# Local attention: 128-token transposes split into two 64-token ones on the halves of the array's rows, both groups beside the mask, one shared pair of banks

## The reference

```
qkv = shift_tokens(x) @ Wqkv;  q, k, v = split(qkv)
q, k = rope(l2norm(q) * qs), rope(l2norm(k) * ksc)       # per head
sim = q @ k.T * 8, each window of 32 queries sees its own and the previous window
out = softmax(masked sim) @ v;  x = out @ Wo + x
x = (a * gelu(gate)) @ W2 + b2 + x,  a, gate = layernorm(shift_tokens(x)) @ W1 + b1
```

## Time and profile before

| | us |
|---|---|
| median of 3 runs | 5310.74 (5309.5 to 5312.04) |
| profiled execution, span from first to last instruction | 5297.4 |
| TensorE busy | 4675.9 (88%) |
| DVE busy | 4003.6 (76%) |
| ACT busy | 3636.0 (69%) |
| POOL busy | 2657.4 (50%) |

### The profile page before, as it was taken

How to read it: one execution, slowest core, us unless ns; L and a number is a source line. 1 busy time by engine, 2 the same in 40 slices (tenths; PEclk the granted TensorE clock), 3 DMA queues, 4 the chain that set the end, 5 groups by cost and what they waited for, 6 DMA issues and landing times. The chain is left out here.

```text
span 5297.4 us, 148317 instructions
## 1 busy us (share of the span) xinstructions
PE 4675.9 (88%) x45796; PEld 2897.7 (55%) x45796; DVE 4003.6 (76%) x8097; ACT 3636.0 (69%) x11780; POOL 2657.4 (50%) x2108
## 2 busy tenths in 40 slices
PE   5999999698898998989989767989989989899897
PEld 1333332366565665656656544665656656566565
DVE  7888886587786877868778546878868778687785
ACT  1777777586785876858768514867858778587684
POOL 3000000465665666656656404656656566566564
PEclk6999999899999999999999977999999999999998
DMA  0000000222222222222222302222222222222223
GB/s 13 1 2 1 2 1 1 85 59 72 59 59 77 59 71 60 59 77 59 64 66 60 83 7 85 59 73 59 57 78 59 72 62 57 77 60 69 65 56 93
DMA packets 332305, 288.20 MB, mean 54 GB/s; under 512 B 149102, under 2 KB 290964, under 8 KB 329748
## 3 DMA queue, kind: packets, MB, share of 16 engines
q1 hardware_dynamic: 331028, 281.93, 20.6%
q10 hardware_dynamic: 768, 0.02, 0.0%
HBM read 100.42 MB, written 30.41 MB: 25 GB/s over the span
## 5 line engine op out<-in xcount | busy, mean ns | idle before, releaser
L929 POOL TENSOR_TENSOR g_rn<-g_ss,g_minus_half 128x8 f32<-128x8 f32 x384 | 636.8, 1658 | 299.7 <-DVE g_ss L1077 297.0
L929 POOL TENSOR_TENSOR f_rn<-f_ss,f_minus_half 128x8 f32<-128x8 f32 x384 | 636.8, 1658 | 299.2 <-DVE f_ss L1077 295.9
L425 DVE TENSOR_REDUCE a_maxima<-a_max 128x1 f32<-128x512 f32 x1024 | 651.3, 685 | 148.4 <-PE a_max L539 142.2
L1003 ACT ACTIVATE f_ex<-f_bank,f_nmx 128x96 f32<-128x96 f32 x1536 | 501.5, 338 | 226.8 <-DVE f_nmx L1082 226.8
L1003 ACT ACTIVATE g_ex<-g_bank,g_nmx 128x96 f32<-128x96 f32 x1536 | 501.6, 338 | 226.6 <-DVE g_nmx L1082 226.6
L349 ACT ACTIVATE a_pex<-a_scores 128x512 f32<-128x512 f32 x1024 | 531.7, 607 | 159.6 <-PE a_scores L548 159.6
L934 POOL TENSOR_TENSOR f_qr<-f_t 128x512 f32<-128x512 f32 x384 | 488.4, 1272 | 268.8 <-DVE f_t L1100 268.8
L934 POOL TENSOR_TENSOR g_qr<-g_t 128x512 f32<-128x512 f32 x384 | 488.2, 1271 | 269.0 <-DVE g_t L1100 269.0
L1172 PE MATMUL g_bank<-g_wqkv,g_xT 128*128 128x512 f32 x768 | 407.2, 613 | 30.4 <-ACT g_xT L977 24.3
L1172 PE MATMUL f_bank<-f_wqkv,f_xT 128*128 128x512 f32 x768 | 406.4, 612 | 29.2 <-ACT f_xT L977 24.5
L1077 DVE TENSOR_REDUCE g_ss<-g_sq 128x8 f32<-128x512 f32 x384 | 263.1, 685 | 207.9 <-ACT g_sq L985 207.9
(11 more groups left out here) (244 smaller groups left out, 11909.8 us busy)
## 6 DMA issues: line engine op xcount, KB each, us to landing
f_vw<-f_vt SPq DMA_DIRECT2D x96, 384.0 KB, 4.3
g_vw<-g_vt SPq DMA_DIRECT2D x96, 384.0 KB, 4.3
f_vw<-f_vt SPq DMA_DIRECT2D x96, 256.0 KB, 3.5
g_vw<-g_vt SPq DMA_DIRECT2D x96, 256.0 KB, 3.5
f_vw<-f_vt SPq DMA_DIRECT2D x96, 128.0 KB, 2.3
g_vw<-g_vt SPq DMA_DIRECT2D x96, 128.0 KB, 2.3
f_wqkv<-in_f_Wqkv_dram SPq DMA_DIRECT2D x7, 1536.0 KB, 9.5
g_wqkv<-in_f_Wqkv_dram SPq DMA_DIRECT2D x7, 1536.0 KB, 9.3
```

The lines of the kernel that those rows point to most:

```text
L425: dve.tensor_reduce(maxima[:, m // 4, m % 4:m % 4 + 1], ps_max[m % 3][:], AX.X, ALU.max).then_inc(dv_max, 1)
L929: pool.tensor_tensor(rn[:, b, :], ss[:, b, :], minus_half[:], ALU.pow).then_inc(pl_rn, 1)
L1003: last = act.activation(ex[:, b, u, :], ps_s[:, h, KEYS * jj:KEYS * jj + KEYS], ACT.Exp, bias=nmx[:, b, u:u + 1], accum_out=sm[:, b, u:u + 1])
```

## The change

A transpose of 128 tokens becomes two of 64 tokens, one on rows 0 to 63 of the array, one on rows 64 to 127, each into its own bank: banks 3 and 4 become one tile `ps_T` of two banks, whose columns 0 to 255 take the qr transposes and 256 to 511 the pn transposes. ACT's copies put the halves together by their access patterns. On TensorE the output projection moves ahead of the transposes, and both groups of transposes stand directly before the mask; on ACT both copies stand before the exps. Since both groups share banks, each waits for both of ACT's earlier copies, and the pT copy waits for the qr transposes of its step.

```diff
-        one = [bank(i) for i in range(6)]
+        one = [bank(i) for i in range(3)]
+        ps_T = bank(3, 2)
+        last_one = bank(5)
-        ps_qkT = banks[3]
-        ps_pT = banks[4]
+        ps_qkT = ps_T[:, :, 0:256]
+        ps_pT = ps_T[:, :, 256:512]
+        def made(t, c, lag):
+            return min(4 * t + c - lag, STEPS - 1) if isinstance(t, int) else 4 * t + c - lag
 # ACT, in a step: square, [v copy], and then
+                    if real(t, c, 6):
+                        act.wait_ge(pe_pT, upto(pe_pT, L, n - 6))
+                        act.wait_ge(pe_qkT, upto(pe_qkT, L, made(t, c, 2)))
+                        act.wait_ge(pe_o, upto(pe_o, L, n - 8))
+                        act.copy(pT[0:KEYS, b, :, :].rearrange("p u (r q) -> p r u q", r=2),
+                                 ps_pT[0:KEYS].rearrange("p r (u q) -> p r u q", u=4)).then_inc(act_pT, 1)
+                    if real(t, c, 2):
...
+                        turned = ps_qkT.rearrange("p r (j q) -> p r j q", j=4)
+                            act.copy(qT[:, pairs, :].rearrange("p j (r q) -> p r j q", r=2), turned).then_inc(act_qk, 1)
...
                     if c == 1 and real(t + 1, 0, 0):
                         put_xT(L, t + 1, 1 - q)
                     if real(t, c, 4):
...
-                    if real(t, c, 2):
...
 # TensorE, in a step: L1172, [L1161], [L1189], and then
+                    if c == 3 and real(t - 2, 0, 0):
...
+                            last = pe.matmul(ps_y[:, 0:P], aT[:, q, j, :], wo[:, j, :], start=(j == 0), stop=(j == PAIRS - 1))
+                        last.then_inc(pe_Wo, 1)
+                    if real(t, c, 6):
+                        pe.wait_ge(dv_pn, upto(dv_pn, L, n - 6))
+                        pe.wait_ge(act_pT, upto(act_pT, L, n - 7))
+                        pe.wait_ge(act_qk, upto(act_qk, L, made(t, c, 3))).then_inc(own["pe"], 1)
+                        for u in range(4):
+                            for half in range(2):
+                                r = slice(BLK * half, BLK * half + BLK)
+                                last = pe.transpose(ps_pT[0:KEYS, half, BLK * u:BLK * u + BLK], pn[r, b, u, :], ident[r, r],
+                                                    tile_position=(BLK * half, 0))
+                        last.then_inc(pe_pT, 1)
+                    if real(t, c, 2):
+                        pe.wait_ge(pl_qr, upto(pl_qr, L, n - 2))
+                        pe.wait_ge(act_qk, upto(act_qk, L, n - 3))
+                        pe.wait_ge(act_pT, upto(act_pT, L, n - 7)).then_inc(own["pe"], 1)
+                        for j in range(4):
+                            for half in range(2):
+                                r = slice(BLK * half, BLK * half + BLK)
+                                last = pe.transpose(ps_qkT[:, half, BLK * j:BLK * j + BLK], qr[r, b, P * j:P * j + P], ident[r, r],
+                                                    tile_position=(BLK * half, 0))
+                        last.then_inc(pe_qkT, 1)
                     if real(t, c, 4):
 # mask, scores, values; then
-                    if c == 3 and real(t - 2, 0, 0):
...
-                    if real(t, c, 2):
...
 # feed-forward group 1 on TensorE
+                    pe.wait_ge(act_pT, upto(act_pT, L, STEPS - 1))
```

More of the change, by code:

```diff
@@ L650, in bank @@
             return ctx.enter_context(nc.psum_tensor(f"{tag}_bank{i}", [P, n, 512], F32))
-        one = [bank(i) for i in range(6)]
+        one = [bank(i) for i in range(3)]
+        ps_T = bank(3, 2)
+        last_one = bank(5)
         ps_s = bank(6, 2)
-        banks = [t[:, 0, :] for t in one] + [ps_s[:, 0, :], ps_s[:, 1, :]]
+        banks = [t[:, 0, :] for t in one] + [ps_T[:, 0, :], ps_T[:, 1, :], last_one[:, 0, :], ps_s[:, 0, :], ps_s[:, 1, :]]
         ps_qk = banks[0:2]
         ps_v = banks[2]
-        ps_qkT = banks[3]
-        ps_pT = banks[4]
+        ps_qkT = ps_T[:, :, 0:256]
+        ps_pT = ps_T[:, :, 256:512]
         ps_o = banks[5]
@@ L738, in local_stack @@
         pe_s, dv_max, act_exp = sem("pe_s", STEPS, 4), sem("dv_max", STEPS), sem("act_exp", STEPS, 2)
-        dv_rd, dv_pn, pe_pT, act_pT = sem("dv_rd", STEPS), sem("dv_pn", STEPS, 2), sem("pe_pT", STEPS, 2), sem("act_pT", STEPS, 1)
+        dv_rd, dv_pn, pe_pT, act_pT = sem("dv_rd", STEPS), sem("dv_pn", STEPS, 2), sem("pe_pT", STEPS, 2), sem("act_pT", STEPS, 5)
         pe_o, act_aT = sem("pe_o", STEPS, 8), sem("act_aT", STEPS, 1)
@@ L985, in tile @@
                         act.activation(sq[:, b, :], ps_qk[b][:], ACT.Square).then_inc(act_sq, 1)
[L986 to L989, removed]
                     if c % 2 == 0 and real(t, c, 0):
@@ L995, in tile @@
                         act.copy(vt[:, q, 512 * half:512 * half + 512], ps_v[:]).then_inc(act_v, 1)
+                    if real(t, c, 6):
[5 more added lines that the diff above has]
+                    if real(t, c, 2):
+                        tj, cj = t + (c - 2) // 4, (c - 2) % 4
+                        pairs = slice(4 * HALF[cj], 4 * HALF[cj] + 4)
+                        turned = ps_qkT.rearrange("p r (j q) -> p r j q", j=4)
+                        act.wait_ge(pe_qkT, upto(pe_qkT, L, n - 2))
+                        act.wait_ge(pe_s, upto(pe_s, L, 4 * tj - 3 + 2 * HALF[cj]))
+                        if KIND[cj] == 0:
+                            act.copy(qT[:, pairs, :].rearrange("p j (r q) -> p r j q", r=2), turned).then_inc(act_qk, 1)
+                        else:
+                            act.copy(kT[:, pairs, 0:WINDOW], kT[:, pairs, P:P + WINDOW]).then_inc(act_kprev, 1)
+                            act.wait_ge(act_kprev, upto(act_kprev, L, 2 * tj + HALF[cj]))
+                            act.copy(kT[:, pairs, WINDOW:].rearrange("p j (r q) -> p r j q", r=2), turned).then_inc(act_qk, 1)
                     if c == 1 and real(t + 1, 0, 0):
@@ L1172, in tile @@
                         pe.matmul(ps_qk[b][:], xT[:, q, :], wqkv[:, at:at + 512], start=True, stop=True).then_inc(pe_qkv, 1)
[L1173 to L1178, removed]
                     if c == 1 and real(t + 1, 0, 0):
@@ L1189, in tile @@
                         pe.matmul(ps_v[:], xT[:, q, :], wqkv[:, at:at + 512], start=True, stop=True).then_inc(pe_v, 1)
+                    if c == 3 and real(t - 2, 0, 0):
+                        pe.wait_ge(act_aT, upto(act_aT, L, 4 * t - 5))
+                        pe.wait_ge(act_v, upto(act_v, L, min(2 * t, 2 * NT - 2) + 1 if known else 2 * t + 1))
+                        pe.wait_ge(dv_y, upto(dv_y, L, t - 3))
+                        for j in range(PAIRS):
+                            last = pe.matmul(ps_y[:, 0:P], aT[:, q, j, :], wo[:, j, :], start=(j == 0), stop=(j == PAIRS - 1))
[20 more added lines that the diff above has]
+                        last.then_inc(pe_qkT, 1)
                     if real(t, c, 4):
```

## The result

The changed kernel takes 6204.04 us (median of four, 6195.86 to 6211.75) against 5310.12 for the kernel before on the same chip: ratio 1.169, 95% interval 1.168 to 1.171. The forecast was 6144 (6030 to 6500). The profiled execution has a span of 6193.8 us, 896.4 above the 5297.4 of before.

What follows compares the result with a forecast made beforehand. A ring through DVE, POOL and TensorE bounds each step at 4.83+0.35=5.18 us; 61 steps plus 14x0.64 make 325.0 for 255.0 us a layer, 833 us in twelve: span 6130, timed 6144 us (6030 to 6500).

Steps and rivals of the forecast that it cites:

- The ring: Each loop step holds row maximum, rope products, qr, transposes, scores, next maximum: 4.83+q, 5.18 us a step; chance 0.76.
- q: Time of the eight half qr transposes on TensorE in each step, taken as 0.35 us between bounds 0.22 and 0.94.
- mask to maximum: Stretch of each step from TensorE's mask start to DVE's next row maximum, put at 0.91 us.
- the 5.1 to 5.3: Sign of a right forecast: row maxima 5.1 to 5.3 us apart, near 5.8 every fourth.
- the low bound of 0.22: Eight half qr transposes with half the columns on both array halves at once: 0.22 us, giving 6035 us in all.
- the rival without overlap: The transposes' row halves do not overlap on TensorE: group 0.7 to 0.94 us, total 6440 to 6670 us; chance 0.08.
- The step with the output projection: Projection, waiting for ACT's aT, stands before the transposes: 0.64 us longer than other steps, in 14 of 61 intervals.
- The step behind it: Value projection waits for DVE's residual add; with pn ends at 4.0 against 3.92 us, costed at nothing; if late, 0.1.
- The 61 intervals: Steps between row maxima in a layer, forecast to take 325.0 us with the projection extra, in place of 255.0.
- The rival with 0.10: TensorE's granted clock falls as it idles more: 6680 us with half the steps slow, up to 7216; chance 0.10.
- the full case: Clock at 0.50 throughout: the ring's transposes, mask and scores and the output projection double, 1072 us more, 7216.
- the last two intervals: Maxima after the 62nd in each layer, in steps without qr transposes; no added time was forecast for them.

## Why the prediction was right

**The ring.** Shown: the order alone brings it, a longer group lengthens every step by its own 0.25 us, a shorter way for the sum shortens it by 0.62 (4.99 to 4.37), and moving the group back ends it. Its terms, forecast and read: maximum to the products' end 2.44 and 2.44; hand-over and sum 1.35 and 1.34; hand-over to TensorE 0.13 and 0.11; q 0.35 and 0.27; mask to maximum 0.91 and 0.83. Sum 5.18 and 4.99. So plain steps lie under the 5.1 to 5.3 that the prediction named as its sign, and over the 4.8 that would have refuted it. The two terms that were set too long are the group and the stretch from the mask to the maximum; why the latter is 0.83 in one step and 0.94 in the one behind the residual (mask 1200.53, maximum 1201.47) was not followed up.

**The row halves.** q lies near the low bound of 0.22, so the rival without overlap is out. The figure of the Trainium skill ("TensorEngine Tiling (Array Packing)", Theoretical Speedup), up to twice, is reached beside the mask: 0.27 against 0.59 for the unsplit group in the same place, and against the 0.47 of before. The first is a little over twice, the second 1.7 times. The same page of the Trainium skill says (Key Properties) that changing the tiling mode drains the array; the 0.36 to 0.39 of the groups away from the mask fit that, though no run here measures the drain by itself.

**The step with the output projection.** Forecast 5.82, read 5.80, with the wait for ACT's aT 0.93 us before L1199 as described. Two errors cancel in it: L1199 starts 2.53 us after the maximum (forecast 2.37) and takes 1.95 (1.89), while the qr group and the way from the mask to the maximum take 1.06 (1.26). **The step behind it** was costed as level and is 0.21 longer: TensorE waits 0.92 us for the residual before L1192, starts it 2.69 us after the maximum, and reaches the qr group at 4.01 (1221.60) in place of 3.89: the 0.1 that the prediction named as the price if it were late. The other 0.1 lies between mask and maximum.

**The count.** The maximum at 1262.62 is the 61st of its layer and not the 62nd; 64 stand from 1007.63 to 1272.18. The 61 intervals took 257.9 us, not 255.0. After, they take 323.7 (1010.37 to 1334.04); the forecast was 324.3. So the measured growth is 65.8 us in this layer, the forecast 69.3. In all twelve layers the intervals grew by 797 us, not 833: 36 less, nearly all of it the wrong count.

**The clock.** The rival with 0.10 came true in small: 0.896 in the mean of the run and 0.89 in one of the stretches of 60 us, just under the 0.9 that the prediction named as this rival's sign. (Before, it was 0.957 in the mean; a 9 in the page's row of slices is 90% or more and not 1.00.) The run with more pn work puts its price at 80 us, against the 1072 that the prediction gave for the full case. In the full loop of stack f it lengthens plain steps of c = 1 and c = 2 alone, up to 6.1 us, while the step with the output projection stays at 5.8. The rival had named the steps without value or output projection, which is c = 1, but had priced the output projection as slowed too.

**What was left out.** Beside the 797 us of the intervals the span grew by 99 us that the prediction put at nothing. 50 of them are the last two intervals of each layer, 6.6 us before and 10.2 to 11.2 after; all of it is in the last one, which goes from 2.95 to 6.8 us and more. The prediction passed over them because no qr transposes stand there, but the output projection stands there a fifteenth time, and it too moved ahead of the mask. In the first layer it waits for aT and lasts 3.44 us start to start (1339.81 to 1343.25) in place of 1.95, at the low clock; before the change it stood behind the scores.

```profile
1339.81 3.51 PE L1199 MATMUL f_bank<-f_wo,f_aT 128*128 128x128 f32 x16 [1.40 <-ACT f_aT L1034]
```

Another 36 lie between the last maximum of a layer and the first of the next, and 13 outside the stacks' maxima; these were not followed up.

**Luck.** The mechanism is the forecast one, but that the sum lies only 60 us low (6144 against 6204) is partly luck. With the thin step filled, so nearly without the low clock, the 732 intervals take 3837 us; the forecast was 3892, and the changed kernel takes 3892 because the low clock, which the forecast put at nothing, gives back what the ring's terms were set too long. The wrong count took 36 us off and the terms left out put 99 on: 63 in the span, less 3 because the median lies 10.2 over the profiled span and not 13.3.

## What to carry to other kernels

Before moving a group within an in-order queue, write down which item each engine handles in a step and follow the path through all queues: moving the transposes ahead of the scores with the split saved 0.37 us of TensorE a step (0.43+0.47 to 0.26+0.27) and closed a ring through three engines, in which every step pays the sum of all hand-overs. Look for all arms of the ring, not only the longest; shortening one brought out the other. Follow the moved work to the end of the loop too, where the last steps have other neighbours. Here the small array tiles paid beside work of the same tiling and hardly elsewhere (0.26 and 0.27 against 0.36 and 0.39 us a group), and shared banks turn a copy of one group into a wait of the other.

## What the hardware did that was not expected

- A DVE product of two SBUF tiles (pn, 0.56 us) took 1.63 us when POOL's sum of two SBUF tiles had started 0.05 us ahead of it; median 1.636 over the 384 of a stack, and 0.56 with the sum on DVE. Beside POOL's sum in the changed kernel DVE's L1080 and L1086 kept 0.68: each of them has one input in SBUF. The Trainium skill ("SBUF — State Buffer", SBUF: two separate sides) describes it: DVE's ops with two SBUF inputs and POOL share a port pair that is locked for a whole instruction. The rows agree in the main: DVE's end, 1209.09, is 0.42 after POOL's, 1208.67, where pn alone takes 0.56.
- 1.04 us a tile of useless transposes made the kernel 80 us faster, with the granted clock in the loop at 1.00.
